# Layer planes stored once in DRAM and repeated by the loads, with all instruction lists of a two-layer attention kernel rewritten

## The reference

```python
# layer 0, on each image
ll, lh, hl, hh = haar(x)                      # 32 x 32 each, high = (lh, hl, hh)
q, k, v = conv1x1(ll, qkv_w)                  # 8 heads of 16 channels, N = 1024
q, k = q / |q|, k / |k|
attn = q k^T * 16**-0.5                       # 1024 x 1024 a head
attn = where(attn in top 512 of its row, attn, -1e9)
ll_out = group_norm(conv1x1(softmax(attn) v, proj_w))
high_out = high + alpha * group_norm(conv1x1(silu(group_norm(dwconv3x3(high)))))
out = x + 0.1 * inverse_haar(ll + ll_out, high_out)
out = out + 0.1 * group_norm(conv1x1(gelu(group_norm(conv1x1(out, w1))), w2))
# layer 1, on each image, n = 4096
q, k = Wq x + bq, Wk x + bk                   # 16 channels
out = gamma * (Wo (Wv x + bv) softmax(q k^T / 4)^T + bo) + x
```

## Time and profile before

| | |
|---|---|
| median of 3 runs | 5668.78 us (5662.02 to 5674.28) |
| span of the profiled execution | 5667.7 us |
| PE, DVE, ACT busy | 4766.2, 4618.9, 4256.4 us |
| DMA | 199.97 MB, 104805 packets |
| mean granted TensorE clock | 0.912 |

### The profile page before, as it was taken

The page is one execution under the profiler, slowest core; times in us unless marked ns, Lnnn a source line. Parts: engine busy times, 40 slices in busy tenths (PEclk is TensorE's granted clock), DMA queues, the critical chain, the costliest instruction groups (busy, mean ns, idle before and its releaser), DMA issues.

```text
span 5667.7 us, 92692 instructions
## 1 busy us (share of the span) xinstructions
PE 4766.2 (84%) x30180; PEld 3123.3 (55%) x30180; DVE 4618.9 (81%) x9087; ACT 4256.4 (75%) x6779; POOL 250.6 (4%) x125
## 2 busy tenths in 40 slices
PE   4444899988999889988999889998899889997799
PEld 2001366654666456663666546664466636664588
DVE  4887799987999789986999879997799879996553
ACT  3883699948998499966999489884899669994333
POOL 2001000010000200010000100002000100000000
PEclk7555799998999989998999989999899989998899
DMA  1001200012001110012000120011100120001100
GB/s 68 7 11 50 74 15 16 15 56 76 16 20 43 59 43 18 16 61 74 15 15 13 58 76 16 20 43 50 51 16 18 59 75 15 15 13 43 36 12 16
DMA packets 104805, 199.97 MB, mean 35 GB/s; under 512 B 36632, under 2 KB 41656, under 8 KB 100184
## 3 DMA queue, kind: packets, MB, share of 16 engines
q1 hardware_dynamic: 104280, 193.56, 11.1%
HBM read 110.61 MB, written 82.05 MB: 34 GB/s over the span
## 4 chain that ended last, share of the span: by engine, by line
PE 41%; DVE 23%; ACT 15%; issue 14%; SPq 3%; DMA 3%; DVEq 0%; ACTq 0%; POOL 0%; POOLq 0%
PE PS L582 16%; ACT work L1183 7%; PE PS L548 5%; DVE M L1760 4%; DVE MX L1928 4%; PE PS L566 4%; ACT work L1243 3%; DVE work L1751 3%; PE PS L514 3%; PE PS L524 3%; DVE work L1743 2%; PE PS L1057 2%; ACT arena L1175 2%; DVE arena L1857 2%; DMA work<-TPT 1%
## 5 line engine op out<-in xcount | busy, mean ns | idle before, releaser
L582 PEld LDWEIGHTS PS<-V,work 128*128 128x128 f32 x16384 | 2106.7, 193 | 155.8 <-issue 7.0
L582 PE MATMUL PS<-V,work 128*128 128x129 f32 x16384 | 2125.2, 277 | 2.5 <-ACT work L1243 1.2
L1183 ACT ACTIVATE work<-arena,T 128x1024 bf16<-128x1024 f32 x1504 | 1725.8, 1150 | 22.7 <-DVE T L1671 18.8
L1928 DVE TENSOR_REDUCE MX<-PS 128x1 f32<-128x512 f32 x2048 | 1399.3, 687 | 249.6 <-PE PS L548 233.9
L1243 ACT ACTIVATE work<-PS 128x1024 f32<-128x1024 f32 x1024 | 1046.8, 1024 | 334.0 <-PE PS L566 332.3
L548 PE MATMUL PS<-KP,QP 96*128 96x512 bf16 x2048 | 845.5, 414 | 137.3 <-DVE MX L1928 95.3
L566 PE MATMUL PS<-QP,KP 99*128 99x512 bf16 x2048 | 624.6, 387 | 77.5 <-ACT work L1243 54.2
L1175 ACT ACTIVATE arena<-PS 128x1024 f32<-128x1024 f32 x512 | 523.2, 1022 | 216.7 <-PE PS L446 209.5
L1857 DVE SCALAR_TENSOR_TENSOR arena<-PS,work 128x512 f32<-128x512 f32 x896 | 606.2, 684 | 67.3 <-ACT work L1235 65.3
L1760 DVE MAX8 M<-work 128x8 f32<-128x512 f32 x1024 | 648.4, 682 | 1.0
L1235 ACT ACTIVATE work<-PS 128x512 f32<-128x512 f32 x896 | 530.8, 601 | 119.9 <-PE PS L514 116.1
(11 more groups left out here) (193 smaller groups left out, 4160.8 us busy)
## 6 DMA issues: line engine op xcount, KB each, us to landing
scr<-work SPq DMA_DIRECT2D x96, 256.0 KB
work<-scr SPq DMA_DIRECT2D x128, 192.0 KB, 2.8
work<-in_x SPq DMA_DIRECT2D x16, 1024.0 KB, 7.7
arena<-in_x SPq DMA_DIRECT2D x8, 2048.0 KB, 9.9
scrX<-arena SPq DMA_DIRECT2D x8, 2048.0 KB, 14.2
XR<-scrX SPq DMA_DIRECT2D x64, 256.0 KB, 2.8
out<-YO SPq DMA_DIRECT2D x64, 256.0 KB, 2.0
scrL<-work SPq DMA_DIRECT2D x24, 512.0 KB, 2.6
```

What stands on the lines that cost most here:

```text
L582: last = mm(PS[:, 5 + i // 2, 136 * (i % 2):136 * (i % 2) + 129], P1[:, (16 * j + k) % 3, t, 128 * i:128 * i + 128], V1[:, mt, :], start=( ...
L1183: A(junk[:, m % 2, :], scores(h, i), ACT.Sign, scale=-1.0, bias=T[:, h % 2, i:i + 1], accum_out=CA[:, h % 2, i:i + 1]).then_inc(s["ca"], 1)
L1928: V.reduce_max(MX[:, c % 2, i, w:w + 1], PS[:, maxbank(c, k, l0), :], AX.X).then_inc(s["mr"], 1)
```

## The change

The planes of layer 0 are stored as they lie, once each. A head's 96 rows are now put together by seven loads, of which those of repeated planes read the same rows two or three times (`to_broadcast`, or planes 0 and 1 as one transfer). TERMS gets another order so that equal planes of q lie together. Head 0 is loaded in parts: planes 0 and 1 before plane 2 is stored, plane 2 straight from SBUF. In layer 1 the store puts the four column blocks of a plane into rows of 4096, each plane as soon as it exists, and seven loads fill QP1 and KP1.

```diff
-TERMS = [(0, 0), (0, 1), (1, 0), (1, 1), (0, 2), (2, 0)]
+TERMS = [(0, 0), (0, 1), (0, 2), (1, 0), (1, 1), (2, 0)]
-        scr0 = nc.dram_tensor("scr0", [2, NH, len(TERMS), HD, N0], bf16, kind="Internal").ap()
-        scr1 = nc.dram_tensor("scr1", [3, 128, N0], bf16, kind="Internal").ap()
+        scr0 = nc.dram_tensor("scr0", [3, 128, 2, N0], bf16, kind="Internal").ap()
+        scr1 = nc.dram_tensor("scr1", [3, 32, N1], bf16, kind="Internal").ap()
-            def load_head(h):
+            def load_head(h, parts=(0, 1, 2)):
                 done = s["hq%d" % (h % 3)]
-                for w in range(2):
-                    sp.dma_start(QK0[0:KS, h % 3, w, :], scr0[w, h].rearrange("j d n -> (j d) n")).then_inc(done, 16)
+                d = slice(HD * h, HD * h + HD)
+                q, k = QK0[0:KS, h % 3, 0, :], QK0[0:KS, h % 3, 1, :]
+                if 0 in parts:
+                    sp.dma_start(q[0:48], scr0[0, d, 0, :].unsqueeze(0).to_broadcast([3, HD, N0])).then_inc(done, 16)
+                    sp.dma_start(k[80:96], scr0[0, d, 1, :]).then_inc(done, 16)
+                if 1 in parts:
+                    sp.dma_start(k[0:32], scr0[0:2, d, 1, :]).then_inc(done, 16)
+                    sp.dma_start(k[48:80], scr0[0:2, d, 1, :]).then_inc(done, 16)
+                    sp.dma_start(q[48:80], scr0[1, d, 0, :].unsqueeze(0).to_broadcast([2, HD, N0])).then_inc(done, 16)
+                if 2 in parts:
+                    sp.dma_start(q[80:96], scr0[2, d, 0, :]).then_inc(done, 16)
+                    sp.dma_start(k[32:48], scr0[2, d, 1, :]).then_inc(done, 16)
-            def store_planes(n, t, made):
+            def store_plane(n, t, made):
                 sp.wait_ge(s[made], (n + 1) * 2)
-                for j, pair in enumerate(TERMS):
-                    for w in range(2):
-                        if pair[w] == t:
-                            sp.dma_start(scr0[w, :, j, :, :], PT[:, t, w * N0:w * N0 + N0]).then_inc(s["scrw"], 16)
+                sp.dma_start(scr0[t].rearrange("p w n -> p (w n)"), PT[:, t, :]).then_inc(s["scrw"], 16)
+            def head0_late():
+                for w, row in ((0, 80), (1, 32)):
+                    sp.dma_start(QK0[row:row + HD, 0, w, :], PT[0:HD, 2, w * N0:w * N0 + N0]).then_inc(s["hq0"], 16)
...
                 if opn:
-                    store_planes(n, 0, "p0")
-                    store_planes(n, 1, "p1")
-                    store_planes(n, 2, "p2")
+                    store_plane(n, 0, "p0")
+                    store_plane(n, 1, "p1")
                     sp.wait_ge(s["vt"], (n + 1) * 2)
                     sp.sem_inc(s["free"], 1)
-                    sp.wait_ge(s["scrw"], (n + 1) * 192)
-                    for h in range(3):
+                    sp.wait_ge(s["scrw"], n * 48 + 32)
+                    load_head(0, (0, 1))
+                    store_plane(n, 2, "p2")
+                    head0_late()
+                    sp.wait_ge(s["scrw"], (n + 1) * 48)
+                    for h in range(1, 3):
                         load_head(h)
                 if fin:
-                    sp.wait_ge(s["p12"], f + 1)
-                    for a in range(3):
-                        sp.dma_start(scr1[a], PT1[:, a, :]).then_inc(s["scrw1"], 16)
-                    sp.wait_ge(s["scrw1"], (f + 1) * 48)
-                    for j, (tq, tk) in enumerate(TERMS):
-                        for w, (t, dst) in enumerate(((tq, QP1), (tk, KP1))):
-                            sp.dma_start(dst[16 * j:16 * j + 16].rearrange("p (j n) -> p j n", j=4),
-                                         scr1[t].rearrange("(j s) n -> s j n", s=32)[16 * w:16 * w + 16]).then_inc(s["qp1"], 16)
+                    for a, made in enumerate(("p10", "p11", "p12")):
+                        sp.wait_ge(s[made], f + 1)
+                        sp.dma_start(scr1[a].rearrange("s (j n) -> j s n", j=4), PT1[:, a, :]).then_inc(s["scrw1" if a < 2 else "scry1"], 16)
+                    sp.wait_ge(s["scrw1"], (f + 1) * 32)
+                    planes = scr1.rearrange("t (w d) n -> t w d n", w=2)
+                    sp.dma_start(KP1[0:32], planes[0:2, 1]).then_inc(s["qp1"], 16)
+                    sp.dma_start(KP1[48:80], planes[0:2, 1]).then_inc(s["qp1"], 16)
+                    sp.dma_start(KP1[80:96], planes[0, 1]).then_inc(s["qp1"], 16)
+                    sp.dma_start(QP1[0:48], planes[0, 0].unsqueeze(0).to_broadcast([3, HD, N1])).then_inc(s["qp1"], 16)
+                    sp.dma_start(QP1[48:80], planes[1, 0].unsqueeze(0).to_broadcast([2, HD, N1])).then_inc(s["qp1"], 16)
+                    sp.wait_ge(s["scry1"], (f + 1) * 16)
+                    sp.dma_start(KP1[32:48], planes[2, 1]).then_inc(s["qp1"], 16)
+                    sp.dma_start(QP1[80:96], planes[2, 0]).then_inc(s["qp1"], 16)
```

More of the change, by code:

```diff
@@ L435, in _ @@
             for i in range(3):
-                sp.wait_ge(s["hq%d" % i], images * len(range(i, NH, 3)) * 32)
+                sp.wait_ge(s["hq%d" % i], images * len(range(i, NH, 3)) * 112)
             sp.wait_ge(s["dls"], images * 48)
@@ L654, in search @@
-                    l1_weigh(h - 1, 2, (0,))
+                    l1_weigh(h - 1, 2, (1,))
+                    l1_score(h - 1, 4)
                     maxima(h, 7)
-                    l1_weigh(h - 1, 2, (1,))
+                    l1_weigh(h - 1, 3, (0,))
+                    maxima(h, 8)
                     score(h, 7)
-                    l1_score(h - 1, 4)
-                    maxima(h, 8)
-                    maxima(h, 9)
-                    l1_weigh(h - 1, 3, (0,))
-                    maxima(h, 10)
@@ L669, in search @@
                     l1_score(h - 1, 7)
-                    l1_weigh(h - 1, 5, (0,))
-                    maxima(h, 12)
-                    l1_weigh(h - 1, 5, (1,))
-                    l1_score(h - 1, 8)
+                    l1_weigh(h - 1, 6, (1,))
+                    l1_weigh(h - 1, 7, (0,))
                     found_sum(h - 1)
                     maxima(h, 13)
-                    l1_weigh(h - 1, 6, (0,))
+                    l1_weigh(h - 1, 7, (1,))
+                    l1_score(h - 1, 8)
@@ L720, in search @@
+                    half_t(h - 1, 4, 1)
                     half_t(h - 1, 5, 0)
                     l1_score(h - 1, 13)
-                    maxima(h, 28)
+                    maxima(h, 29)
+                    l1_weigh(h - 1, 12, (0,))
+                    weigh(h - 1, 2)
+                    maxima(h, 30)
                     half_t(h - 1, 5, 1)
-                    l1_weigh(h - 1, 12, (0,))
-                    maxima(h, 29)
+                    l1_score(h - 1, 14)
                     l1_weigh(h - 1, 12, (1,))
+                    maxima(h, 31)
@@ L763, in closing @@
                     l1_weigh(NH - 1, 6, (1,))
+                    found_sum(NH - 1)
                     l1_score(NH - 1, 8)
+                    l1_weigh(NH - 1, 7, (0,))
+                    turn(NH - 1)
                     l1_score(NH - 1, 9)
-                    l1_weigh(NH - 1, 7, (0,))
-                    found_sum(NH - 1)
                     l1_weigh(NH - 1, 7, (1,))
                     l1_weigh(NH - 1, 8, (0,))
-                    turn(NH - 1)
+                    l1_score(NH - 1, 10)
@@ L803, in closing @@
-                    half_t(NH - 1, 6, 0)
-                    l1_weigh(NH - 1, 13, (1,))
-                    half_t(NH - 1, 6, 1)
-                    l1_score(NH - 1, 15)
-                    l1_weigh(NH - 1, 14, (0,))
-                    l1_weigh(NH - 1, 14, (1,))
-                    half_t(NH - 1, 7, 0)
+                    l1_score(NH - 1, 12)
+                    half_t(NH - 1, 3, 0)
+                    l1_weigh(NH - 1, 11, (0,))
+                    half_t(NH - 1, 3, 1)
+                    l1_score(NH - 1, 13)
@@ new lines, in closing @@
+                    l1_weigh(NH - 1, 11, (1,))
+                    l1_weigh(NH - 1, 12, (0,))
+                    half_t(NH - 1, 4, 0)
+                    half_t(NH - 1, 4, 1)
+                    l1_score(NH - 1, 14)
+                    l1_weigh(NH - 1, 12, (1,))
+                    l1_weigh(NH - 1, 13, (0,))
+                    half_t(NH - 1, 5, 0)
+                    weigh(NH - 1, 1)
+                    l1_score(NH - 1, 15)
+                    l1_weigh(NH - 1, 13, (1,))
+                    half_t(NH - 1, 5, 1)
@@ L2232, in alone @@
                         count(h + 1, 1, 6)
+                        update(h + 1, 1, 0)
+                        base(h - 1, 2)
+                        count(h + 1, 1, 7)
                         base(h, 0)
                         based(h - 1)
-                        update(h + 1, 1, 0)
+                        head_out(h - 1)
+                        update(h + 1, 1, 1)
                         mask(h, 0)
+                        mask(h, 1)
                         sums(h - 1)
-                        count(h + 1, 1, 7)
-                        mask(h, 1)
-                        update(h + 1, 1, 1)
```

594 lines of the change are left out of this document (285 added, 309 removed).

## The result

The changed kernel takes 5760.6 us (median of 4 runs, 5758.9 to 5761.7) against 5665.4 us before: the ratio is 1.0173, interval 1.0154 to 1.0191. That is +95 us where +58 was forecast, inside the forecast's own range (5685 to 5775). The profiled execution has a span of 5758.1 us, 90.4 more than before.

The account below looks back on a forecast made before the run. PE, DVE and ACT run close to full in slots; the stretch between images was taken to decide. 98 + 7 - 25 - 12 - 10 = +58 us gave 5727 us, own range 5685 to 5775, overall 5600 to 5800.

Parts of the forecast that it names:

- Late loads: Between images: QP1/KP1 loads end at 1352 against 1338.2, 14 us a time, 98 us over 7 images; chance 0.60.
- I take 1311: Between images: the loads of heads 1 and 2 can start at 1311, once plane 2 has landed, near the old 1309.9.
- that of two plane stores at 1327.5, plus 1 us: Between images: the line of two layer 1 plane stores ends at 1327.5, plus 1 us to be seen, before the loads.
- 21.8 us of loads and 1 us: Between images: four QP1/KP1 loads put 524 kB on one same engine, 21.8 us, then 1 us more.
- the loads are not late: Rival: narrow loads use different engines or all 16 and land before V1's last copy; -74, 5595 us; chance 0.20.
- After the last image: After image 7: stores landed by 5272.5, loads done at 5295.5 against 5288.6, 7 us later.
- Slots: Slots with both layers: half_m and l1_weigh fill waits around TPT; -0.6 us a slot, 42 slots, -25 us.
- Image 0: Image 0 alone: count(2, 0) and centre(1) move ahead, -1.5 us a head, 8 heads, -12 us.
- Closing: Closing of an image: threshold() ahead of two mixes, base 1 to 3 between last masks; -1.5, 7 times, -10 us.
- Plane stores: Layer 0 plane stores: 12 become 3, 15.7 us become 4 us, SP freed about 12 us; gain costed at nothing.
- The lists win more: Rival: loads late as forecast, but slots give -80 and the others -52; sum -27, 5641 us; chance 0.10.
- The lists lose: Rival: a wait of 1 us a slot on maxima behind a full PE, +42 for -25, 5794 us; chance 0.10.

Follow-up runs that it names:

- run 7: Changed kernel with transfers in parts of 16 or 32 rows, layer 1 planes early, heads 1 and 2 loaded behind layer 1's loads: 5579.2 us.
- run 6: Changed kernel with the loads of heads 1 and 2 issued behind the stores and loads of layer 1: 5721.9 us.
- 11: Changed kernel's own narrow transfers, with layer 1 planes early and heads 1 and 2 issued behind layer 1's loads: 5696.0 us.
- 12: Changed kernel with planes early, heads 1 and 2 behind layer 1's loads, each layer 1 plane store in four parts of 32 rows, narrow loads kept: 5659.4 us.
- run 8: Changed kernel with the store of X1 held back until the loads of KP1 and QP1 have landed: 5765.4 us.
- run 1: Changed kernel's new lists with the transfers, layouts and TERMS of the kernel before: 5669.1 us.
- run 3: New lists with the old transfers, and the three planes of layer 1 as early as before: 5609.3 us.
- run 4: Changed kernel with each transfer between the images in parts of 16 or 32 rows, layouts and lists as changed: 5626.9 us.
- runs 9: Kernel before with the new first(), search() and closing() lists, but PE's old order at the turn of a slot: 5684.2 us.
- run 10: Kernel before with the new first(), search() and closing() lists and PE's new order at the turn of a slot: 5633.0 us.
- run 5: Changed kernel with thirteen groups of transfers ahead of image 0, each waited for: 5899 us, groups included.

## Why the forecast was right in its mechanism and short in its size

**Late loads: right mechanism, the term was mis-sized.** "That is 14 us a time, over 7 images 98 us" measured 21.4 us a time and 150 us. The load stretch of the changed kernel is 22.8 us above that of run 7, and the runs divide it: 4.7 us heads 1 and 2 ahead of layer 1 (run 6), 4.7 planes late in the lists (runs 6 and 11), 4.5 stores of 4 parts (12), 8.9 narrow loads (12 against 7). (The forecast's own steps add up to 1351.3 and not 1352, so to 13.1 us a time and 92 us: it was a little further off than it says.) The steps, on the clock of the profiles, on which qk1 stands 2.1 us earlier in the changed kernel (1307.9 against 1310.0), so each is that much later than its time says: "I take 1311" for the head loads was 1312.9, because plane 2's store stood behind head 0's narrow loads; "that of two plane stores at 1327.5, plus 1 us" was 1332.6, because all three stores went out together (SP was busy with 14 issues when the first two planes existed) and each puts 65.5 kB on the same four engines; "21.8 us of loads and 1 us" was 25.6. The loads by themselves take 20.6, so some 3 to 4 us between their issue and PE's release stay unexplained; the store of X1 was the suspect, and run 8 cleared it.

**Luck.** The losses were 59 us more than forecast, the gains 28 us more, and the two errors partly cancel. The loss alone would have led to 5786 us, outside the forecast's own range; most of the gain that brought it back came from chunk 7's slot, which the forecast had not priced.

**The same term hid a second one.** The forecast saw that centre0(0) delays plane 2 and costed it at nothing beside the late loads; that ACT's part1(0) now stands behind evict0(0), which waits for PE, and PE for head 0, it did not see. With the old transfers the two places cost 8.0 us an image and all that the lists win (runs 1 and 3), with the narrow ones behind a good queue 4.7 us. So the rival "the loads are not late" was priced too low at 5595: without a narrow transfer the time is 5669 (run 1) or 5627 us (run 4), until the planes are moved.

**After the last image**: 7 us forecast, 14.3 measured, of the same two causes: 10.0 us from the first store's issue to the loads' issue where 5.8 were taken, 26.2 to PE's release where 22.8 were.

**Slots**: -25 forecast, -46 measured, and not where it was looked for. The six full slots brought 14 us instead of 25; chunk 7's slot brought 29, which the forecast had no term for. The cause given, half_m and l1_weigh around TPT, is not shown: in runs 9 and 10 the six slots lose without PE's new order at the turn of a slot, which the forecast did not cost, and win with it. Why slot 1 lost is open.

**Image 0**: -12 forecast, -11.0 measured. **Closing**: -10 forecast, -17.6 measured with the stretch behind it, of which run 10 shows that the new closing() alone brings nothing; it needs the new between(). **Plane stores**, costed at a gain of nothing: the load stretch shows no gain by them, but it did matter for head 0. PE waited for its planes 7.7 us in the kernel before, 58.8 us with the new lists and the old transfers (run 1), 28.0 us in the changed kernel (eight waits, below) and 9.6 us with the wide parts of run 4. So the new lists bring this wait, and the early load of head 0 takes back part of it; in its narrow form less than in the wide one.

```profile
PE PS L465 <- DMA work<-work: 28.0, 8, 4.7
```

**Rivals.** "The loads are not late" fell with the 25 us in which PE waits for QP1, and with run 5: a share of 0.11 for two loads of 2 parts at once. (By the letter of the forecast, a share above 0.5 during the loads was to prove it wrong, and from 1338 to 1346 it is 0.97. That was the store of X1: without it, in run 8, the share is 0.16.) The Trainium skill, page "DMA: Bandwidth & Descriptors", section "Why a DMA increments its semaphore by 16 and not by 1", has the rule for how many engines carry a DMA from SP and that they are the lowest-numbered ones; run 5 agrees for 2 parts (0.11 to 0.13), 4 (0.22) and, less closely, 12 (0.69) and 16 (0.84). That these groups are too short to be at full share all the time is an argument, not shown. "The lists win more" is true of the gains as a whole, and did not decide. "The lists lose" did not come in the slots; between the images they lose 9.5 us a time with the old transfers, 66 us in all, for a reason that it did not name.

## What to carry to other kernels

Cost a transfer by the number of parts of its outermost dimension and by who stands on the same engines, not by its bytes; but measure the form that would replace it as well, since one that keeps all engines busy can still be slow (here 12.8 us for 1.6 MB). When a chain of DMAs becomes critical, follow it up to the engine that makes its first operand and look at what each in-order list has in front of that instruction: here three operations moved in lists of hundreds were worth 60 us (run 3 against run 1). And when a set of lists is rewritten, time its pieces, since some of them may do nothing or harm while another carries the gain.

## What the runs showed of the hardware that I had not expected

- Twelve loads of 16 rows each (1.6 MB) take 12.8 us at a share of 0.98 to 1.05, whether the pieces are 8 KB or 2 KB, while one load of 96 rows in 16 parts moves 218 GB/s. The engines were busy and slow. One load of 16 rows alone took 0.6 us (131 kB, some 210 GB/s), which speaks against the 16 rows of the destination as the cause, but it is too short to rule them out; the cause stays open.
- Loads of 3, 5 and 6 parts that read the same 16 rows took 9 us each, where two loads of 2 parts with rows of their own took 11.0 together, 5.5 each. Each part is 131 kB in all of them, so the engines went slower (41 GB/s with three parts), perhaps because they read the same addresses; that wasn't tried apart.
- SP's issue took much longer in one place: in run 11 the 14 head loads behind the four narrow loads took SP 24.5 us to issue (one of them alone 9.2 us) instead of 8.8. In its trace the row is `1326.97 9.16 SPq L286 DMA_DIRECT2D work<-scr  x1`. What exactly held SP wasn't tried.
